# A chunked scan with a feed-forward block: turns as PE transposes, one turn of the keys, and the down products and v's projection placed differently

## The chip, the cores and the metric

The kernel runs on one core of one Trainium2 chip. The metric is the device time in microseconds (us), the median of several executions; lower is better.

## What is computed

```python
x = x + layernorm(attn(layernorm(x)))           # x: 2048 x 512, float32
x = x + layernorm(ffn(layernorm(x)))
# attn: 16 heads of 32; chunks of 16 tokens, one after the other, with a state S (32 x 32 per head)
q = silu(x @ Wq); k = normalised(x @ Wk); v = x @ Wv; beta = 2 * sigmoid(x @ Wbeta)
def step(S, (qi, ki, vi, ei)):
    kh = ki @ S;  kh_hat = normalised(kh);  g = w * kh_hat + b - (vi - ki)
    v_new = (g*w - mean(g*w) - kh_hat * mean(g*w * kh_hat)) * rstd
    A = tril(qi @ ki.T) * ei
    o = qi + layernorm(qi @ S - A @ v_new)
    S = S - (ki * ei).T @ v_new
o = normalised(o * sigmoid(x @ Wg1 @ Wg2)) * norm_w;  attn = o @ Wo
# ffn: weights rounded to float8_e4m3, I = 1536
ffn = ((silu((x @ gate_w) * gs) * ((x @ up_w) * us)) @ down_w) * ds
```

## The kernel before

The 2048 tokens are 16 tiles of 128 rows. A tile holds 8 chunks of the scan in a form where all heads of a chunk are computed at once, so the scan is 128 chunks in a row, each needing the state of the one before. `body(t, s, h)` is one tile; s is t's parity and h = t // 2. Each engine has its own copy of `body` with the order of its work written out by hand, chunk by chunk (j = 0 to 7). In tile t the kernel runs tile t's scan, the preparation of tile t + 1 (`prep_*`), what follows the scan for tile t - 1 (`post_*`) and t - 2 (`tail_*`), and the feed-forward block for pairs of tiles (`pair_*`, `ffn_*`, `fin_*`). A pair has 6 rounds; each tile from the fourth on does three (numbers 0, 1 and 2 in `ffn`). A round is `ffn_g` (gate, bank G), `ffn_u` in two parts (up, bank U4), silu on ScalarE (ACT), the product f and its high and low halves fh and fl, and then `ffn_down` for k = 0 and k = 1, one per tile of the pair, each of four matmuls of 512 columns (L587). After tile 15, five more passes through `body` drain the pipeline.

In each chunk TensorE (PE) does `read_state` (L491 and L500), then some other work, then `write_state` (L514 and L522), then some more other work. Between the read and the write VectorE (DVE) and GpSimd (POOL) compute v_new: statistics (L1254), a power on POOL (L1000), and in the end VX (L1290). PE's write waits for VX. DVE adds the state S (L1297) once L514 is done, and the next read waits for S. DVE's other work stands behind VX, ahead of S ("front" places), and behind S.

PE's other work, by chunk, before the change:

- j = 0: read; down k = 1 of the last tile's round 1; the turn of xn; gate and up of round 0; write; up, second part.
- j = 1: read; q; down k = 0 of the last tile's round 2; write; its down k = 1.
- j = 2: read; in odd tiles the two turns of the pair (`pair_xT`); k; write; the turn of q.
- j = 3: read; gate and up of round 1; write; up, second part.
- j = 4: read; v; write; down k = 0 of round 0.
- j = 5: read; down k = 1 of round 0; two turns of the keys; gate of round 2; write; `prep_beta` (L413 and L397).
- j = 6: read; the turn of d; up of round 2; the gate projection (L420); write; `prep_cen` (L426).
- j = 7: read; `post_wo` (L537); write; down k = 0 of round 1; `prep_brow` (L426).

A turn (`turn`, L405) is a 128 x 512 tile turned block by block: eight matmuls against the identity, each 64 output columns wide, four for each half of the array. The projections, the read and the write are in the same 64-wide form; the feed-forward matmuls (L554, L587) are 128 wide. The trace has two records for each float32 matmul of a turn or a projection (x16 for a turn) and one for each feed-forward matmul.

The keys are turned twice, into PA[0] ("kT2") and PA[1] ("kT1"). DVE turns PA[0] once more into kR (`prep_kR`, L1199), in front place of j = 5. ACT copies PA[1] into BDk in two halves (`prep_BDk`, L755): the first in j = 5 ahead of the chunk's output copy (`take_qh`, L810), the second behind fh (L704), the gate copies (L719 and L704) and bt (L729). PE's turn of d waits for bt. ACT's rT (L778) comes later, and `prep_cen` waits for it. v is projected into PA[1]; `prep_d` (L1216) reads it, after kn (L1210). In tiles 0 to 4 DVE, ACT and POOL also round the feed-forward weights, one unit per chunk (L1392 to L1402, L860, L862, L1086).

Of the kernel before, what the change touches and what calls it, by code (L numbers as in the profile page):

```python
# [14 lines left out]
P = 128  # L15
T, D = 2048, 512
# [63 lines left out]
def begun(n):  # L80

    return not isinstance(n, int) or n >= 0


def build(nc, x, wq, wk, wv, wo, wbeta, wg1, wg2, norm_w, ln_w, ln_b, gate_w, up_w, down_w,
# [15 lines left out]
    with ctx:  # L101
# [7 lines left out]
        Wq, Wk, Wv, Wo = (sb(n, KD * D) for n in ("Wq", "Wk", "Wv", "Wo"))  # L109
# [11 lines left out]
        ident = cst[:, C_ID:C_ID + P]  # L121
# [7 lines left out]
        qT, qR, thR = ([sb(f"{n}{s}", D) for s in range(2)] for n in ("qT", "qR", "thR"))  # L129
        rR, kR = sb("rR", D), sb("kR", D)  # L130
# [9 lines left out]
        Pw, u, g, t_ = (work[:, 64 * n:64 * (n + 1)] for n in range(4))  # L140
# [36 lines left out]
        PA, G, U4, Y = bank[2:4], bank[4], bank[5], bank[6:8]  # L177
# [20 lines left out]
        prep_v = Each(sem, "prep_v", "kss qR kn d kR bx rR em er eM thR")  # L198
        prep_a = Each(sem, "prep_a", "xnT q ksq qT g1 beta BDk rT th")
        prep_t = Each(sem, "prep_t", "xnT q k qT v kT2 kT1 g1 beta dT gate cen brow")  # L200
# [80 lines left out]
        def half_done(t, s, h):  # L281

            p, r = (h - 2, 3) if s else (h - 2, 0)
            return [(p, r)] if is_pair(p) else []
# [99 lines left out]
        def _(pe):  # L384
            mm = nc.tensor.matmul


            HALVES = (slice(0, 64), slice(64, P))

            def half(t, block, lo):  # L390

                return t[:, block * P + lo.start:block * P + lo.stop]

            def proj(dst, W, n, blocks=range(KD)):
                for k in blocks:
                    for lo in HALVES:
                        ins = mm(dst[lo, :], half(xnT, k, lo), W[:, k * n:(k + 1) * n],  # L397
                                 start=(k == 0), stop=(k == KD - 1), skip_group_check=True)
                return ins

            def turn(dst, src, one):

                for g in range(4):
                    for lo in HALVES:
                        ins = mm(dst[lo, g * P:(g + 1) * P], half(src, g, lo), ident, start=True, stop=True,  # L405
                                 skip_group_check=True)
                ins.then_inc(*one)

            def gate_in(b):

                for k in range(KD):
                    for lo in HALVES:
                        ins = mm(b[lo, 0:64], Wgb[:, k * DG:k * DG + 64], half(xnT, k, lo),  # L413
# [24 lines left out]
                proj(PA[0][:, :], Wq, D).then_inc(*prep_t.one("q"))  # L438

            def prep_beta(t):  # L440
                pe.wait_ge(*prep_v.at("kR", t))
                gate_in(PA[0])
                proj(PA[0][:, P:P + H], Wb, H).then_inc(*prep_t.one("beta"))

# [7 lines left out]

                turn(PA[1], qtok, prep_t.one("qT"))

            def prep_vv(t):
                pe.wait_ge(*prep_v.at("qR", t))
                proj(PA[1][:, :], Wv, D).then_inc(*prep_t.one("v"))

            def prep_kT(t):
                pe.wait_ge(*prep_v.at("d", t))  # L460
                turn(PA[0], kn, prep_t.one("kT2"))
                turn(PA[1], kn, prep_t.one("kT1"))

            def prep_dT(t):
# [12 lines left out]
            def prep_brow(t):  # L477
                pe.wait_ge(*prep_v.at("rR", t))
                fixed(PA[0][:, 0:P], C_REP, bx[:, :], prep_t.one("brow"))
# [97 lines left out]
            def ffn_down(p, r, k):  # L577
                if k == 0:
                    pe.wait_ge(*low(p, r))
                    if p == 0:  # L580
                        pe.wait_ge(*quantized(r // 2, 12))
                    if r == 0 and p > 0:
                        pe.wait_ge(fin_v.sem, fin_v.at("y1", p - 1))
                for q in range(RM):
                    m = RM * r + q
                    for part in (fh, fl):
                        ins = mm(Y[k][:, :], part[:, q * PAIR + k * P:q * PAIR + (k + 1) * P], DW[:, m * D:(m + 1) * D],  # L587
                                 start=(m == 0 and part is fh), stop=(m == MI - 1 and part is fl))
                if k == 1:
                    ins.then_inc(*down_t.one("dn"))  # L590

            def body(t, s, h):
                norm, prep, scan, post, tail = live(t)
                o = 1 - s
                ffn = rounds(t, s, h)
                for j in range(NC):
                    if scan:
                        read_state(t, j, s)

                    if j == 0:  # L600
                        for p, r in half_done(t, s, h):
                            ffn_down(p, r, 1)
                        if prep:
                            prep_xnT(t + 1)
                        if 0 in ffn:
                            ffn_g(*ffn[0])
                            ffn_u(*ffn[0], 0)
                    if j == 1:
                        if prep:
                            prep_q(t + 1)  # L610
                        for p, r in left_over(t, s, h):
                            ffn_down(p, r, 0)
                    if j == 2:
                        if s and is_pair(h - 1):
                            pair_xT(h - 1)
                        if prep:
                            prep_k(t + 1)
                    if j == 3 and 1 in ffn:
                        ffn_g(*ffn[1])
                        ffn_u(*ffn[1], 0)  # L620
                    if j == 4 and prep:
                        prep_vv(t + 1)
                    if j == 5:
                        if 0 in ffn:
                            ffn_down(*ffn[0], 1)
                        if prep:
                            prep_kT(t + 1)
                        if 2 in ffn:
                            ffn_g(*ffn[2])
                    if j == 6:  # L630
                        if prep:
                            prep_dT(t + 1)
                        if 2 in ffn:
                            ffn_u(*ffn[2], 0)
                            ffn_u(*ffn[2], 1)
                        if prep:
                            prep_gate(t + 1)
                    if j == 7 and post:
                        post_wo(t - 1)
                    if scan:  # L640
                        write_state(t, j, s)

                    if j == 0 and 0 in ffn:
                        ffn_u(*ffn[0], 1)
                    if j == 1:
                        for p, r in left_over(t, s, h):
                            ffn_down(p, r, 1)
                    if j == 2 and prep:
                        prep_qT(t + 1)
                    if j == 3 and 1 in ffn:  # L650
                        ffn_u(*ffn[1], 1)
                    if j == 4 and 0 in ffn:
                        ffn_down(*ffn[0], 0)
                    if j == 5 and prep:
                        prep_beta(t + 1)
                    if j == 6 and prep:
                        prep_cen(t + 1)
                    if j == 7:
                        if 1 in ffn:
                            ffn_down(*ffn[1], 0)  # L660
                        if prep:
                            prep_brow(t + 1)

            def prologue():

# [34 lines left out]
        def _(act):  # L700
# [44 lines left out]
            def prep_BDk(t, s, a):  # L745

                if a == 0:
                    act.wait_ge(*prep_t.at("kT1", t))
                    if begun(NC * (t - 1) - 1):
                        act.wait_ge(scan_t.sem, scan_t.at("kh", NC * (t - 1) - 1))  # L750
                for h in (2 * a, 2 * a + 1):
                    q = slice(32 * h, 32 * h + 32)
                    for gp in range(2):
                        p = 64 * gp + 32 * (h % 2)
                        ins = fn(bdk(s)[q, :, gp, own(h)],  # L755
                                 PA[1][p:p + 32, 256 * a:256 * a + 256].rearrange("p (m c) -> p m c", c=CH), ACT.Copy)
                if a or t == 0:
                    ins.then_inc(*prep_a.one("BDk"))
# [407 lines left out]
        def _(dve):  # L1166
# [30 lines left out]
            def turn(dst, src, one):  # L1197

                nc.vector.transpose(rows(dst), feat(src)).then_inc(*one)  # L1199
# [16 lines left out]
                tt(dv[:, :], kn[:, :], PA[1][:, :], ALU.subtract).then_inc(*prep_v.one("d"))  # L1216

            def prep_kR(t, s):
                dve.wait_ge(*prep_t.at("kT2", t))
                if begun(t - 1):  # L1220
                    dve.wait_ge(kdiag_a.sem, kdiag_a.at("k3", t - 1))
                turn(kR, PA[0], prep_v.one("kR"))

            def prep_rR(t, s, b=PA[0]):
                dve.wait_ge(*prep_t.at("cen", t))
# [383 lines left out]
```

## Time and profile before

| what | value |
|---|---|
| median of 3 runs | 943.51 us (943.5 to 944.17) |
| the profiled execution | 944.36 us, span 942.60 us |
| PE busy | 840.1 us, 89% of the span |
| DVE, ACT, POOL busy | 670.3, 505.2, 482.6 us |
| chain that ended last | PE 63%, DVE 17%, POOL 10%, ACT 5%, issue 4% |
| mean granted TensorE clock | 0.959 |

The span is that of the profiled execution, from the first to the last instruction. In a timeline row the columns are the start, the length from the first start to the last end of what was merged, engine, line, operation, output<-inputs, shape and count; in brackets stands how long the engine was idle before it and what released it. Matmuls overlap, so the time from one start to the next is what counts, not a record's length. The L514 row of a chunk is its write, the L491 row its read.

### The profile page before, as it was taken

To read this page: it belongs to the slowest core of one execution; us is meant where nothing else is said; L and a number is where in the kernel's file an instruction comes from. 1 tells how busy PE (TensorE), PEld (TensorE's weight loads), DVE (VectorE), ACT (ScalarE), POOL (GpSimd) and SP (SyncE) were. 2 spreads that over 40 slices of the span, in tenths; PEclk is the share of its full clock that TensorE was granted. 3 is DMA by queue.
4 is the path that set the end of the run, shared out by engine and by line. 5 is a ranking of instruction groups with operands and counts; after the bars stand their busy time and mean duration, and the time that the engine had idled before them with its cause. 6 is when DMAs were issued, how large, how long until landed. Compare 5 with 4: busy or idle time off the path is not lost.

```text
span 942.6 us, 25277 instructions
## 1 busy us (share of the span) xinstructions
PE 840.1 (89%) x9472; PEld 595.6 (63%) x9472; DVE 670.3 (71%) x2695; ACT 505.2 (54%) x1330; POOL 482.6 (51%) x858
## 2 busy tenths in 40 slices
PE   6777676688989999999999999999999999979795
PEld 2444343456567676677576776766676767667594
DVE  2587887978877778677776777677876777767332
ACT  1667575766646565554556464655555564633222
POOL 4355645565554646455555546464555546436312
PEclk9897888989989999999999999999999999989998
DMA  7011121111200001000100010000100010001000
GB/s 257 15 53 48 46 69 34 53 51 35 68 13 24 2 2 46 6 20 2 45 2 24 1 45 4 25 2 2 47 2 24 2 46 2 2 2 45 1 23 23
DMA packets 16730, 28.63 MB, mean 30 GB/s; under 512 B 3520, under 2 KB 3520, under 8 KB 16608
## 3 DMA queue, kind: packets, MB, share of 16 engines
q1 hardware_dynamic: 16608, 27.02, 8.9%
q8 instruction: 75, 1.23, 0.5%
q14 instruction: 47, 0.39, 0.1%
HBM read 22.82 MB, written 4.19 MB: 29 GB/s over the span
## 4 chain that ended last, share of the span: by engine, by line
PE 63%; DVE 17%; POOL 10%; ACT 5%; issue 4%; DMA 0%; POOLq 0%; DVEq 0%; ACTq 0%
PE bank L554 16%; PE bank L397 14%; PE bank L587 9%; PE bank L405 7%; PE bank L514 4%; PE bank L537 4%; POOL rho L1000 3%; PE bank L491 2%; PE bank L522 2%; PE bank L500 2%; DVE work L1281 2%; PE bank L426 1%; DVE work L1285 1%; PE bank L420 1%; DVE VX L1290 1%
## 5 line engine op out<-in xcount | busy, mean ns | idle before, releaser
L1000 POOL TENSOR_TENSOR rho<-sy,cst 128x2 f32<-128x2 f32 x128 | 89.7, 701 | 284.9 <-DVE sy L1254 284.9
L1297 DVE TENSOR_TENSOR SQ<-SQ,bank 128x128 f32<-128x128 f32 x128 | 36.8, 288 | 110.4 <-PE bank L514 109.8
L514 PEld LDWEIGHTS bank<-VX,BDkR 128*64 128x64 f32 x1024 | 45.9, 142 | 96.7 <-issue 51.8
L514 PE MATMUL bank<-VX,BDkR 128*64 128x64 f32 x1024 | 57.7, 235 | 49.9 <-DVE VX L1290 48.7
L810 ACT ACTIVATE qhR<-bank 128x64 f32<-128x64 f32 x128 | 28.3, 221 | 112.0 <-PE bank L522 111.8
L587 PE MATMUL bank<-DW,fh 128*128 128x512 f32 x192 | 84.4, 440 | 1.5 <-DVE fl L1364 1.5
L769 ACT ACTIVATE BDkR<-kR,cst 128x128 f32<-128x128 f32 x256 | 81.4, 398 | 0.0
L587 PE MATMUL bank<-DW,fl 128*128 128x512 f32 x192 | 76.3, 397 | 0.0
L1081 POOL TENSOR_TENSOR fl<-f,fh 128x512 fp32r<-128x512 f32 x32 | 45.6, 1425 | 53.0 <-ACT fh L704 32.3
L1276 DVE SCALAR_TENSOR_TENSOR work<-work,rho,rR 128x32 f32<-128x32 f32 x256 | 53.0, 249 | 25.4 <-POOL rho L1000 24.9
L554 PE MATMUL bank<-xh,GW 128*128 128x256 f32 x384 | 66.3, 296 | 2.8 <-DVE xl L1347 2.5
L755 ACT ACTIVATE BDk<-bank 32x256 f32<-32x256 f32 x124 | 46.5, 375 | 41.5 <-PE bank L405 40.1
L554 PE MATMUL bank<-xh,UW 128*128 128x256 f32 x384 | 66.0, 294 | 0.3 <-DVE f L1358 0.3
L397 PE MATMUL bank<-Wq,xnT 128*64 128x512 f32 x256 | 64.3, 647 | 0.0
L491 PEld LDWEIGHTS bank<-SQ,BDk 128*64 128x64 f32 x1024 | 45.7, 142 | 29.5 <-issue 26.3
L554 PE MATMUL bank<-xl,GW 128*128 128x256 f32 x384 | 62.8, 287 | 0.0
L397 PE MATMUL bank<-Wv,xnT 128*64 128x512 f32 x256 | 62.5, 633 | 0.0
L537 PE MATMUL bank<-Wo,o 128*64 128x512 f32 x256 | 59.9, 611 | 2.9 <-DVE o L1329 2.9
L491 PE MATMUL bank<-SQ,BDk 128*64 128x48 f32 x1024 | 55.8, 231 | 6.5 <-DVE SQ L1297 4.7
L397 PE MATMUL bank<-Wk,xnT 128*64 128x512 f32 x256 | 60.5, 616 | 0.7 <-ACT xnT L704 0.7
L554 PE MATMUL bank<-xl,UW 128*128 128x256 f32 x384 | 61.0, 281 | 0.0
L500 PE MATMUL bank<-SQ,BDq 128*64 128x32 f32 x1024 | 53.2, 225 | 7.9 <-ACT qhR L810 6.7
(154 smaller groups left out, 2224.8 us busy)
## 6 DMA issues: line engine op xcount, KB each, us to landing
xt<-in_x SPq DMA_DIRECT2D x16, 256.0 KB, 2.7
x<-in_x SPq DMA_DIRECT2D x16, 256.0 KB, 2.8
out<-x SPq DMA_DIRECT2D x16, 256.0 KB, 2.0
yb<-in_gate_w SPq DMA_DIRECT2D x12, 256.0 KB, 2.7
yb<-in_up_w SPq DMA_DIRECT2D x12, 256.0 KB, 2.7
yb<-in_down_w SPq DMA_DIRECT2D x12, 256.0 KB, 2.6
Wk<-in_wk SPq DMA_DIRECT2D x1, 1024.0 KB, 6.3
Wv<-in_wv SPq DMA_DIRECT2D x1, 1024.0 KB, 8.2
```

What stands on the lines that cost most here:

```text
L397: ins = mm(dst[lo, :], half(xnT, k, lo), W[:, k * n:(k + 1) * n], start=(k == 0), stop=(k == KD - 1), skip_group_check=True)
L405: ins = mm(dst[lo, g * P:(g + 1) * P], half(src, g, lo), ident, start=True, stop=True, skip_group_check=True)
L491: ins = mm(KAv[gp * 64:(gp + 1) * 64, gh, 0:48], bdk(s)[:, gh * NC + j, gp, :], SQv[:, 2 * gh + gp, :], start=True, stop=True, skip_group_ ...
L500: ins = mm(QH[gp * 64:(gp + 1) * 64, gh * DH:(gh + 1) * DH], bdq[:, j // 4, 2 * gp + gh, j % 4, :], S[:, 2 * gh + gp, :], start=(gh == 0), ...
L514: ins = mm(dS[p, e], bdkr[:, gh, j % 4, p], VX[:, e], start=True, stop=True, skip_group_check=True)
L537: ins = mm(PA[1][lo, :], half(ogT, g, lo), Wo[:, g * D:(g + 1) * D], start=(g == 0), stop=(g == 3), skip_group_check=True)
L554: ins = mm(b[:, q * PAIR:(q + 1) * PAIR], W[:, k * I + m * P:k * I + (m + 1) * P], part[:, k * PAIR:(k + 1) * PAIR], start=(part is xh and ...
L587: ins = mm(Y[k][:, :], part[:, q * PAIR + k * P:q * PAIR + (k + 1) * P], DW[:, m * D:(m + 1) * D], start=(m == 0 and part is fh), stop=(m ...
L755: ins = fn(bdk(s)[q, :, gp, own(h)], PA[1][p:p + 32, 256 * a:256 * a + 256].rearrange("p (m c) -> p m c", c=CH), ACT.Copy)
L769: ins = fn(bdkr[:, :, place, h * DH:(h + 1) * DH], kR[:, :].rearrange("p (gh j e) -> p gh j e", gh=2, e=DH)[:, :, js], ACT.Identity, scale ...
L1000: tt(dst, src, cst[:, C_NH:C_NH + n], ALU.pow).then_inc(*one)
L1276: stt(out=g2(g)[:, gh], in0=g2(u)[:, gh], scalar=rho[:, gh:gh + 1], in1=r_j[:, gh, :], op0=ALU.mult, op1=ALU.add).then_inc(*scan_v.one(f"g ...
```

## The change

- `turn` on PE becomes four `transpose` instructions, 128 x 128 each, over the whole array.
- The keys are turned once in the loop, into PA[1]. DVE's `prep_kR` reads PA[1] for t > 0, and ACT's `prep_BDk` waits for kR (t > 0) before its first half. `prep_beta` on PE waits for kn instead of kR. The prologue turns the keys twice as before.
- `ffn_down` k = 0 of round 1 moves from behind the write of j = 7 to behind the read of the next j = 0, directly ahead of k = 1; that of round 0 from behind the write of j = 4 to behind the read of j = 5, ahead of k = 1.
- v's projection takes its first three quarters where it was (j = 4, before the write) and the last one behind the write of j = 4.

```diff
             def turn(dst, src, one):
                 for g in range(4):
-                    for lo in HALVES:
-                        ins = mm(dst[lo, g * P:(g + 1) * P], half(src, g, lo), ident, start=True, stop=True,
-                                 skip_group_check=True)
+                    ins = nc.tensor.transpose(dst[:, g * P:(g + 1) * P], src[:, g * P:(g + 1) * P], ident)
                 ins.then_inc(*one)
...
             def prep_beta(t):
-                pe.wait_ge(*prep_v.at("kR", t))
+                pe.wait_ge(*prep_v.at("kn", t))
...
-            def prep_vv(t):
-                pe.wait_ge(*prep_v.at("qR", t))
-                proj(PA[1][:, :], Wv, D).then_inc(*prep_t.one("v"))
+            def prep_vv(t, last):
+                if last:
+                    proj(PA[1][:, :], Wv, D, (3,)).then_inc(*prep_t.one("v"))
+                else:
+                    pe.wait_ge(*prep_v.at("qR", t))
+                    proj(PA[1][:, :], Wv, D, (0, 1, 2))
             def prep_kT(t):
                 pe.wait_ge(*prep_v.at("d", t))
-                turn(PA[0], kn, prep_t.one("kT2"))
                 turn(PA[1], kn, prep_t.one("kT1"))
...
                     if j == 0:
                         for p, r in half_done(t, s, h):
+                            ffn_down(p, r, 0)
                             ffn_down(p, r, 1)
...
                     if j == 4 and prep:
-                        prep_vv(t + 1)
+                        prep_vv(t + 1, False)
                     if j == 5:
                         if 0 in ffn:
+                            ffn_down(*ffn[0], 0)
                             ffn_down(*ffn[0], 1)
...
-                    if j == 4 and 0 in ffn:
-                        ffn_down(*ffn[0], 0)
+                    if j == 4 and prep:
+                        prep_vv(t + 1, True)
...
-                    if j == 7:
-                        if 1 in ffn:
-                            ffn_down(*ffn[1], 0)
-                        if prep:
-                            prep_brow(t + 1)
+                    if j == 7 and prep:
+                        prep_brow(t + 1)
... ScalarE, prep_BDk
                 if a == 0:
                     act.wait_ge(*prep_t.at("kT1", t))
+                    if t > 0:
+                        act.wait_ge(*prep_v.at("kR", t))
... VectorE
             def prep_kR(t, s):
-                dve.wait_ge(*prep_t.at("kT2", t))
+                dve.wait_ge(*prep_t.at("kT1" if t else "kT2", t))
...
-                turn(kR, PA[0], prep_v.one("kR"))
+                turn(kR, PA[1] if t else PA[0], prep_v.one("kR"))
```

## Rows read from the trace of the kernel before

**Rows 1.** Timeline of PE, tile 9: read and write of chunk 0

```profile
503.36 0.39 PE L491 MATMUL bank<-SQ,BDk 128*64 128x48 f32 x8
...
509.07 0.45 PE L514 MATMUL bank<-VX,BDkR 128*64 128x64 f32 x8
```

**Rows 2.** Timeline, tile 9, chunk 3: VX and the write

```profile
528.67 0.29 DVE L1290 TENSOR_TENSOR VX<-work,re 128x128 f32<-128x128 f32 x1
...
529.02 0.45 PE L514 MATMUL bank<-VX,BDkR 128*64 128x64 f32 x8 [0.57 <-DVE VX L1290]
```

**Rows 3.** Timeline, tile 9: write of chunk 7, state, read of tile 10

```profile
554.11 0.45 PE L514 MATMUL bank<-VX,BDkR 128*64 128x64 f32 x8 [0.32 <-DVE VX L1290]
...
554.61 0.29 DVE L1297 TENSOR_TENSOR SQ<-SQ,bank 128x128 f32<-128x128 f32 x1
...
556.10 0.39 PE L491 MATMUL bank<-SQ,BDk 128*64 128x48 f32 x8
```

**Rows 4.** Timeline of PE, tile 9: write of chunk 2, turn, read

```profile
523.38 0.40 PE L514 MATMUL bank<-VX,BDkR 128*64 128x64 f32 x8
...
523.82 1.07 PE L405 MATMUL bank<-cst,q_kn_th 128*64 128x128 f32 x16
524.72 0.39 PE L491 MATMUL bank<-SQ,BDk 128*64 128x48 f32 x8
```

**Rows 5.** Timeline of PE, tile 9: write of chunk 4, down product, read

```profile
534.70 0.40 PE L514 MATMUL bank<-VX,BDkR 128*64 128x64 f32 x8
...
535.23 0.50 PE L587 MATMUL bank<-DW,fh 128*128 128x512 f32 x1
535.57 0.40 PE L587 MATMUL bank<-DW,fl 128*128 128x512 f32 x1
...
536.04 0.40 PE L587 MATMUL bank<-DW,fl 128*128 128x512 f32 x1
536.37 0.44 PE L491 MATMUL bank<-SQ,BDk 128*64 128x48 f32 x8
```

**Rows 6.** Groups of instructions, PE's weight loads (busy us, mean ns)

```profile
L405 PEld LDWEIGHTS bank<-cst,q_kn_th 128*64 128x64 f32 x768 | 41.6, 137 | 9.0 <-issue 4.0 <-DVE xn_dv_rT L1216 2.7 <-DVE q_kn_th L1515 1.5
L587 PEld LDWEIGHTS bank<-DW,fl 128*128 128x128 f32 x192 | 36.5, 190 | 4.9
```

**Rows 7.** Timeline, tile 9, front of chunk 4: v and VX

```profile
531.23 3.63 PE L397 MATMUL bank<-Wv,xnT 128*64 128x512 f32 x16
...
533.50 0.29 DVE L1290 TENSOR_TENSOR VX<-work,re 128x128 f32<-128x128 f32 x1
```

**Rows 8.** Timeline, tile 9, chunks 4 to 6: keys, ACT's queue, turn of d

```profile
536.07 0.69 DVE L1216 TENSOR_TENSOR xn_dv_rT<-q_kn_th,bank 128x512 f32<-128x512 f32 x1
...
539.70 0.29 DVE L1290 TENSOR_TENSOR VX<-work,re 128x128 f32<-128x128 f32 x1
539.91 0.71 DVE L1199 STREAM_TRANSPOSE kR<-bank 128x512 f32<-128x512 f32 x1
...
540.11 1.54 ACT L755 ACTIVATE BDk<-bank 32x256 f32<-32x256 f32 x4 [3.00 <-PE bank L405]
...
542.88 0.62 ACT L704 ACTIVATE fh<-f 128x512 fp32r<-128x512 f32 x1
...
543.68 0.21 ACT L719 ACTIVATE g1T<-bank 32x64 f32<-32x64 f32 x1 [0.18 <-PE bank L397]
...
544.15 0.18 ACT L729 ACTIVATE bt<-bank 128x16 f32<-128x16 f32 x1
...
544.38 1.09 PE L405 MATMUL bank<-cst,xn_dv_rT 128*64 128x128 f32 x16 [0.27 <-ACT bt L729]
...
548.40 0.40 PE L514 MATMUL bank<-VX,BDkR 128*64 128x64 f32 x8
```

**Rows 9.** Stretches of 10 us: length, PE, PEld, DVE, ACT, POOL, PEclk, DMA share, GB/s

```profile
80.00:90.00 10.00, 7.94 (x65) 4.85 (x64) 8.29 (x37) 6.93 (x17) 5.47 (x9) 0.52 0.25 79
...
820.00:830.00 10.00, 6.46 (x105) 5.08 (x104) 8.21 (x36) 6.82 (x20) 7.44 (x13) 1.00 0.00 1
```

## The prediction, made before the changed kernel was run

> **What bounds the kernel now.** I read the PE timeline of one steady tile first, then the other engines in the same stretch, then the granted clock. Call the time from a chunk's first read matmul (L491) to its first write matmul (L514) its front, and from there to the next read its post; C0 to C7 are the chunks of a tile. Every piece of feed-forward and preparation work sits in a front or a post, so each slot ends either when PE is through or when the scan's own chain is. The mark is in the L514 row: with "<-DVE VX" and an idle time, the chain ended last; with no idle time, PE did. In C0 of tile 9 there is no idle time [rows 1], and none in C4 and C6, whose writes stand further down: PE ends them last. In C3 and C7 PE waited 0.57 and 0.32 us for VX [rows 2, 3]. L514 follows the start of VX by 0.35 us (528.67 to 529.02) [rows 2]. Tile 9 takes 52.7 us (503.36 to 556.10) [rows 1, 3]. It is a chain of slots, so I price the change slot by slot and give a slot only what its other bound allows.
>
> **Unit prices.** A turn in C2's post takes 0.90 us, from 523.82 to the next read at 524.72 [rows 4]. Of a down product (four matmuls) one matmul follows the other in 0.23 us (535.57 to 536.04 is two) [rows 5]. Going from 64-wide to 128-wide work costs something: L514 to the next work is 0.44 us where that is a 64-wide turn (523.38 to 523.82) and 0.53 where it is a down product (534.70 to 535.23), the first down matmul holds 0.34 instead of 0.23, and the last one 0.33 (536.04 to 536.37) [rows 4, 5]. So an excursion into 128-wide work costs 0.09 + 0.11 + 0.10 = 0.30 us beside its work.
>
> **The transposes.** No row shows one. A turn becomes four of them, each a 128-column weight load and 128 moving columns. The load of 64 columns has a record of 137 ns and that of 128 columns one of 190 [rows 6]: 53 ns per 64 columns, so 107 ns for 128, and the rest of a record overlaps. I take one load after the other as the pace: 4 x 0.107 is 0.43, with starts 0.45 us a turn, against 0.90. Lower end: only the streaming counts, a quarter of a down matmul's 0.23 each, 0.23 us a turn. Upper end: nothing overlaps, 4 x (0.19 + 0.06) = 1.0 us. The value nearest a row of the same thing, a 128-column load, is 0.45. The Trainium skill, "TensorE: Matmul & The Clock Gate", Terms, says transpose mode is 4 times faster for FP32. That would be an estimate of 0.22 us a turn and about 901 us in all; I see the load bound as the reason to stay above it, and the sum does not use the page.
>
> **Slot by slot, steady tiles.** Each is after minus before; tau = 0.45 is the turn.
> - *C7 post* loses down k=0 of round 1. 554.11 to 556.10 was 1.99 us; what is left for PE is the write and brow. The state addition S starts 0.50 after the write and takes 0.29 [rows 3], so with the hand-over the floor is about 0.89: -1.10.
> - *C0 front* takes that product: +0.93. Its turn goes from 0.90 to 0.45, and since that turn now is 128-wide, between a down product and gate matmuls, one excursion vanishes, -0.30. Together +0.18. PE ended it last, and stays so. DVE, which waited for brow, gets it earlier: no loss.
> - *C2 front*, odd tiles only: the pair's two turns, 1.80, become 0.90, but stand 128-wide between 64-wide work, +0.30: -0.60. PE ended it last.
> - *C2 post*: one turn shorter, -0.45 + 0.30. I cost it at nothing: C3 ends with VX, and VX hangs on DVE's queue from S on, and in even tiles on the keys' squares; what PE saves it waits for in C3 [rows 2].
> - *C4 front*: v's last quarter goes. v takes 531.23 to 534.70, 3.47 us, a quarter 0.87. The chain allows a write 0.35 after VX starts, 533.85, so 0.85 of it is gained [rows 7]: -0.85. These two bounds are then within 0.02 us of each other.
> - *C4 post to C6 write*, as one stretch of 13.70 us (534.70 to 548.40) [rows 5, 8]. PE's part: the post holds v's quarter, 0.87, instead of a product with an excursion, 1.23: -0.36. C5's front: +0.93 for the product, -1.80 for two turns, +0.45 for one, -0.30 for the excursion: -0.72. So PE could reach dT's turn, which it did 0.27 before 544.38, or 9.41 after the write, at 8.33. But ACT now holds it. **New waits:** d (L1216) started 1.37 us after the write; v's last matmul now ends 0.44 + 0.87 + 0.16 (the record's 3.63 against 3.47) later, so d moves by some 0.1 to 0.15, and with it VX, to 5.15. kR starts 0.21 after VX and takes 0.71; today BDk's first half (540.11) runs beside kR, afterwards it must wait for it: 6.1 instead of 5.41. Behind it on ACT are the output copy, fh, the gate copies and bt: 1.54 for BDk, about 0.1, fh 0.62, then 0.47 from the first gate copy to bt and 0.23 from bt to the turn [rows 8]. dT's turn starts 9.1 after the write, not 9.68: -0.58, and PE idles 0.75 us instead of 0.27. From there on 4.02 us less 0.45: -0.45. The stretch: -1.03. Beta's matmuls now wait for kn instead of kR; kn is over before d starts, so this costs nothing.
> - C0's post, C1, C5's post, C6's post and C7's front keep their times.
>
> An odd and an even tile: 2 x 0.18 - 0.60 - 2 x 1.10 - 2 x 0.85 - 2 x 1.03 = -6.2 us (-3.4 and -2.8). Written with tau it is 6 tau - 8.9. Tiles 5 to 14 are five such pairs: -31.
>
> **The rest.** Tile 4 has no cover for C4 (weights are still being quantised on DVE): 0.18 - 1.03 - 1.10, about -2.0. Tile 3 has the first rounds in it: its C7's post, -1.1, and 0.2 at its turns: -1.3. In tiles 0 to 2 the chain ends the slots; there ACT also works on the quantising, and I add 0.5 each, +1.5, an estimate: the 0.7 by which BDk starts later, less some slack. Tile 15 has no preparation: the product moved into C0 costs 0.93, C4's post gains about 1.1: -0.2. Before the first chunk five turns stand on the path, 5 x 0.45: -2.3. The last pair's two turns, after the scan: -0.9. Sum of these -5.2; all together **-36 us**. The profiled execution took 944.36 us (span 942.60), 0.85 above the median of 943.51; from it the sum gives 908.4, from the median 907.5. I take 907.5.
>
> **Rivals.**
> - *Turns cost what they did* (tau 0.9: full-width, but no cheaper). 5 x (6 x 0.9 - 8.9) = -17.5, and the rest gives -2.9 only, without the prologue's part: 923. Even then one turn and the excursions are gone. For it: nothing in the trace shows a transpose. Against it: half its loads are gone. 0.10.
> - *Only streaming counts* (tau 0.23): 5 x -7.5 = -37.5 and -6: 900. 0.12.
> - *ACT becomes the bound around C5 and C6*: the wait for kR also delays the output copy that C6's second read needs, and everything behind it. If the stretch gives nothing back (1.03 x 11 tiles) and early tiles lose 1 us more each, 907.5 + 11.3 + 3 = 922. 0.07.
> - *Slower: the clock falls in the steady stage.* PE's granted clock is 0.52 in 80 to 90 us, with PE at 7.94 of 10, and 1.00 in 820 to 830 with PE at 6.46 [rows 9]: busy share alone does not tell, but PE would be less busy than today. The two levels are 1.2 and 2.4 GHz; each us of PE work done at the lower one costs a half to one more. In tile 9 PE worked 51.5 us (52.7 less 0.57, 0.32 and 0.27), and the sum takes 4.2 of turns and excursions out: 47.3 in 49.3. The gain is 3.1 a tile, so the change turns into a loss once more than 3.1 us a tile of its work, 6 to 7%, falls to the lower level; with a fifth of each steady tile there it would be 907.5 + 10 x 9.5 = 1002. Against it: those 47.3 of 49.3, with 0.75 us as the longest wait. 0.04. The Trainium skill, "TensorE: Matmul & The Clock Gate", Part 4, says that transposes do not count as PE being busy, which would be this rival's mechanism; a tile has 5 or 6 turns of 0.45 us, never more than two together, with matmuls on both sides.
> - *It all cancels*, within 0.2% (what a measurement of this kernel can tell from no change): 0.02; it would need tau at 1.0 and the ACT bound together.
>
> **How the numbers follow.** The forecast case has 0.65, the rivals 0.10, 0.12, 0.07, 0.04 and 0.02. Its own spread is about 8 us either way, from starts between unlike matmuls and from tiles 0 to 4. The range runs from 897, below the streaming case, to 926, above the 923 and the 922; the end at tau 1.0, 5 x (6 - 8.9) - 2, is 927. Faster 0.94, same 0.02, slower 0.04.
>
> **What the profile of the changed kernel would show.** Turns as records 128*128 128x128, four each, next work 0.45 us later; 81 turns, not 96. A C7 post of 0.9 us; C0's front 5.9; C4's front 3.1; an idle time of 0.7 to 0.8 us ahead of dT's turn "<-ACT bt" for 0.27; BDk starting just after kR; tile 9 in 49.3 us. I am wrong in the turn if that spacing is not 0.4 to 0.5, in the slot model if two tiles don't shorten by 8.9 - 6 tau, and in the whole if PEclk shows less than full speed between 300 and 800 us.

## The result, and the profile after

| | before | changed |
|---|---|---|
| median, us | 943.84 (943.5 to 944.41, 4 runs) | 920.49 (918.7 to 924.58, 4 runs) |
| ratio, 95% interval | 1 | 0.9758 [0.9723, 0.9793] |
| profiled execution, span | 944.36, 942.60 | 919.38, 917.6 |
| mean granted clock | 0.959 | 0.938 |

Faster by 23.4 us where 36 was forecast: the direction and the range held, a third of the gain is missing. The range held for a reason that is partly luck: the forecast case had a spread of 8 us around 907.5, and 920.49 lies outside it; what reaches that far are the ends put there for the rivals at 922 and 923. The page of the changed kernel, parts 1 (busy time), 4 (the chain that ended last) and two groups of part 5:

```profile
PE 797.5 (87%) x8260; PEld 558.3 (61%) x8260; DVE 671.1 (73%) x2695; ACT 500.9 (55%) x1330; POOL 481.6 (52%) x858
...
PE 51%; DVE 20%; POOL 11%; ACT 9%; issue 7%; DMA 1%; SPq 0%; POOLq 0%; DVEq 0%; ACTq 0%
...
L758 ACT ACTIVATE BDk<-bank 32x256 f32<-32x256 f32 x124 | 46.5, 375 | 62.0 <-DVE kR L1202 52.6
...
L502 PE MATMUL bank<-SQ,BDq 128*64 128x32 f32 x1024 | 54.9, 228 | 15.0 <-ACT qhR L813 14.0
```

PE lost 42.6 us of busy time but the program only 25, and PE's share of the last chain fell from 63% to 51%, ACT's rose from 5% to 9%: work left PE and waits on ACT came in. The last two rows name them: BDk waits for kR, as forecast, and PE's second read (L502) waits for qhR, which was not.

**The turn**, answering [rows 4]. Timeline of PE around tile 9's chunk 2, start and length in us:

```profile
509.91 1.09 PE L405 MATMUL bank<-cst,xn 128*128 128x128 f32 x8
510.93 3.65 PE L398 MATMUL bank<-Wk,xnT 128*64 128x512 f32 x16
...
514.42 0.40 PE L516 MATMUL bank<-VX,BDkR 128*64 128x64 f32 x8
...
514.96 0.66 PE L405 MATMUL bank<-cst,q_kn_th 128*128 128x128 f32 x4
515.54 0.44 PE L493 MATMUL bank<-SQ,BDk 128*64 128x48 f32 x8
```

Two turns take 1.02 us to the next 64-wide work and one takes 0.58. The difference is one turn without its excursion: 0.44, and 0.58 - 0.44 = 0.14 is left for leaving 128-wide work; entering it costs 0.54 instead of 0.44 after the write (514.42 to 514.96). So an excursion costs 0.10 + 0.14 = 0.24. Forecast: 0.45 a turn and 0.30 an excursion. The weight loads, answering [rows 6], stretch 300 to 800 us (busy, mean ns):

```profile
L405 PEld LDWEIGHTS bank<-cst,q_kn_th 128*128 128x128 f32 x80 | 9.2, 140 | 1.8
```

The record of a 128-column load is 140 ns here, not the 190 of [rows 6], and the pace is 0.44 / 4 = 0.11 us a transpose. The matmul turn with its 64-column loads kept the same pace: 0.90 / 8 = 0.11 us a step. The transposed turn has half as many steps.

**Chunk 0**, answering [rows 1], PE timeline: tile 9 (odd) and, further down, tile 10 (even) with the write and state before it, answering [rows 3]:

```profile
494.79 0.44 PE L493 MATMUL bank<-SQ,BDk 128*64 128x48 f32 x8
...
500.71 0.45 PE L516 MATMUL bank<-VX,BDkR 128*64 128x64 f32 x8
...
543.24 0.45 PE L516 MATMUL bank<-VX,BDkR 128*64 128x64 f32 x8 [0.32 <-DVE VX L1293]
...
543.74 0.29 DVE L1300 TENSOR_TENSOR SQ<-SQ,bank 128x128 f32<-128x128 f32 x1
...
544.17 0.44 PE L493 MATMUL bank<-SQ,BDk 128*64 128x48 f32 x8
...
544.25 0.19 POOL L1012 TENSOR_TENSOR nb_y<-nm_y,rs_y 128x1 f32<-128x1 f32 x1
...
544.47 0.72 ACT L840 ACTIVATE x<-x,nb_y 128x512 f32<-128x512 f32 x1 [0.46 <-POOL nb_y L1012]
...
545.10 0.20 ACT L813 ACTIVATE qhR<-bank 128x64 f32<-128x64 f32 x1
...
545.45 0.42 PE L502 MATMUL bank<-SQ,BDq 128*64 128x32 f32 x8 [0.84 <-ACT qhR L813]
...
551.13 0.45 PE L516 MATMUL bank<-VX,BDkR 128*64 128x64 f32 x8
```

The post of C7 is 544.17 - 543.24 = 0.93 us, as forecast (0.89). The front of C0 is 5.92 in the odd tile (forecast 5.89) but 6.96 in the even one. In an even tile ACT's queue holds the second half of fin_yc (L840, the pair's closing normalization) ahead of chunk 7's qhR. L840 waits for nb_y on POOL, which ends at 544.44; qhR runs behind it, and PE, whose read now begins 1 us earlier than it used to, stands 0.84 us at L502. The same place before the change, behind the write of 554.11 [rows 3]:

```profile
555.35 0.72 ACT L837 ACTIVATE x<-x,nb_y 128x512 f32<-128x512 f32 x1 [0.46 <-POOL nb_y L1009]
...
555.98 0.20 ACT L810 ACTIVATE qhR<-bank 128x64 f32<-128x64 f32 x1
...
556.33 0.42 PE L500 MATMUL bank<-SQ,BDq 128*64 128x32 f32 x8
```

qhR started 1.87 us after the write before and 1.86 after the change, the second read 2.22 and 2.21. In an even tile nothing of what C7's post gave up was left at the second read.

**Chunks 3 to 6 of tile 9**, timeline of PE, DVE and ACT, answering [rows 2, 5, 7, 8]:

```profile
519.71 0.29 DVE L1293 TENSOR_TENSOR VX<-work,re 128x128 f32<-128x128 f32 x1
...
520.06 0.45 PE L516 MATMUL bank<-VX,BDkR 128*64 128x64 f32 x8 [0.57 <-DVE VX L1293]
...
521.79 0.44 PE L493 MATMUL bank<-SQ,BDk 128*64 128x48 f32 x8
...
524.54 0.29 DVE L1293 TENSOR_TENSOR VX<-work,re 128x128 f32<-128x128 f32 x1
...
524.98 0.45 PE L516 MATMUL bank<-VX,BDkR 128*64 128x64 f32 x8
...
526.33 0.42 PE L493 MATMUL bank<-SQ,BDk 128*64 128x48 f32 x8
...
530.48 0.71 DVE L1202 STREAM_TRANSPOSE kR<-bank 128x512 f32<-128x512 f32 x1
...
531.28 1.53 ACT L758 ACTIVATE BDk<-bank 32x256 f32<-32x256 f32 x4 [4.24 <-DVE kR L1202]
...
533.91 0.18 ACT L730 ACTIVATE bt<-bank 128x16 f32<-128x16 f32 x1
...
534.15 0.66 PE L405 MATMUL bank<-cst,xn_dv_rT 128*128 128x128 f32 x4 [0.62 <-ACT bt L730]
```

C4's front is 3.19 (was 3.95), its post 1.35 (1.67), BDk starts 6.30 after C4's write and 0.09 behind kR's end, and dT's turn starts 9.17 after it, with 0.62 us idle ahead of it (forecast 9.1 and 0.75).

**The clock**, answering [rows 9]. Two stretches of the changed kernel (length, busy PE, PEld, DVE, ACT, POOL, PEclk, DMA share, GB/s), and the first one before, where PEclk was 0.88:

```profile
30.00:250.00 220.00, 159.29 (x1692) 101.32 (x1692) 169.12 (x671) 141.58 (x353) 117.49 (x187) 0.80 0.17 48
...
300.00:800.00 500.00, 480.64 (x5257) 339.23 (x5255) 393.04 (x1662) 285.55 (x807) 279.37 (x523) 1.00 0.06 17
```

```profile
30.00:250.00 220.00, 163.65 (x2020) 107.11 (x2022) 172.42 (x683) 144.27 (x363) 119.02 (x190) 0.88 0.16 49
```

Full in the steady stage, lower in the early tiles. By stretches of the profiled executions, cut at the read of each C0, in us:

| | before | changed | difference | forecast |
|---|---|---|---|---|
| up to the first read | 31.04 | 30.62 | -0.4 | -2.3 |
| tiles 0 to 2 | 152.61 | 156.02 | +3.4 | +1.5 |
| tiles 3, 4 | 55.97, 58.19 | 56.06, 56.70 | +0.1, -1.5 | -1.3, -2.0 |
| tiles 5 to 14 | 514.22 | 489.15 | -25.1 | -31 |
| tile 15 and the end | 130.57 | 129.05 | -1.5 | -1.1 |

### The profile page after: what moved, and what is told of

Read it like the earlier page. It is cut to its first block, busy times and chain, and to the rows that moved or that the text cites. A ratio compares the mean times of both kernels' runs of the same rounds, so it can differ in the third digit from the quotient of the medians.

```text
span 917.6 us, 22854 instructions
## 1 busy us (share of the span) xinstructions
PE 797.5 (87%) x8260; PEld 558.3 (61%) x8260; DVE 671.1 (73%) x2695; ACT 500.9 (55%) x1330; POOL 481.6 (52%) x858
## 3 DMA queue, kind: packets, MB, share of 16 engines
q8 instruction: 65, 1.06, 0.5%
## 4 chain that ended last, share of the span: by engine, by line
PE 51%; DVE 20%; POOL 11%; ACT 9%; issue 7%; DMA 1%; SPq 0%; POOLq 0%; DVEq 0%; ACTq 0%
PE bank L398 14%; PE bank L556 13%; PE bank L589 7%; POOL rho L1003 4%; PE bank L516 4%; PE bank L539 4%; ACT BDk L758 2%; PE bank L405 2%; PE bank L493 2%; DVE work L1284 2%; DVE f L1361 2%; PE bank L502 2%; DVE work L1288 1%; PE bank L524 1%; PE bank L419 1%
## 5 line engine op out<-in xcount | busy, mean ns | idle before, releaser
L589 PE MATMUL bank<-DW,fh 128*128 128x512 f32 x192 | 82.3, 428 | 1.9 <-DVE fl L1367 1.9
L1279 DVE SCALAR_TENSOR_TENSOR work<-work,rho,rR 128x32 f32<-128x32 f32 x256 | 53.0, 249 | 25.6 <-POOL rho L1003 25.1
L502 PE MATMUL bank<-SQ,BDq 128*64 128x32 f32 x1024 | 54.9, 228 | 15.0 <-ACT qhR L813 14.0
L398 PE MATMUL bank<-Wv,xnT 128*64 128x512 f32 x256 | 67.5, 650 | 0.0
```

What stands on the lines that cost most here:

```text
L502: ins = mm(QH[gp * 64:(gp + 1) * 64, gh * DH:(gh + 1) * DH], bdq[:, j // 4, 2 * gp + gh, j % 4, :], S[:, 2 * gh + gp, :], start=(gh == 0), ...
L1279: stt(out=g2(g)[:, gh], in0=g2(u)[:, gh], scalar=rho[:, gh:gh + 1], in1=r_j[:, gh, :], op0=ALU.mult, op1=ALU.add).then_inc(*scan_v.one(f"g ...
```

## The experiments

Ratios are to the kernel before on the same chip, with a 95% interval. Edits are to the changed kernel unless "to before" is said.

**1. Transposes alone** (to before: the turn's body is the changed one, all work where it was).

```
-    for lo in HALVES:
-        ins = mm(dst[lo, g * P:(g + 1) * P], half(src, g, lo), ident, ...)
+    ins = nc.tensor.transpose(dst[:, g * P:(g + 1) * P], src[:, g * P:(g + 1) * P], ident)
```

> The kernel before with its turns as transposes and nothing else changed. Theory (slot sum, with the 0.44 us a turn that the changed kernel shows): C0 -0.75 (turn -0.45, one excursion -0.30), C5 -1.2 (two turns and an excursion), C6 -0.45, C2 -0.6 in odd tiles: 2.7 us a tile, 27 over tiles 5 to 14, 3 to 4 more in tiles 3, 4 and the drain, and the tiles before lose some 2 to 3 us to a lower clock: about 915 us, no slower than the whole change, and no wait of L500 for qhR in C0. Rival A: the gain of 23 us is made by the moves and the single turn of the keys, the transposes being hidden: 935 or more. Rival B: the slot sum holds for the parts, so this gives less than the whole, 922 to 928.

916.71 us (915.38 to 918.03), 0.9714 [0.9698, 0.973]. The transposes alone bring the whole gain of the change: tiles 5 to 14 go from 514.22 to 488.04 us, and the rest of the change makes them 1.1 us longer (489.15). In the steady tiles C5's front went from 5.67 to 4.46 (two turns), C6's from 4.93 to 4.30, and C0's in odd tiles from 5.71 to 5.28. C0 was expected to give 0.75 and gave 0.43, since its write now waits 0.29 us for VX: PE is through before the chain. The down product that the full change moves there partly fills this gap, and C0's front becomes 5.92, 0.64 more and not 0.93.

**2. The moves alone** (the changed kernel's order, each turn as eight 64-wide matmuls again).

```
-    ins = nc.tensor.transpose(dst[:, g * P:(g + 1) * P], src[:, g * P:(g + 1) * P], ident)
+    for lo in HALVES:
+        ins = mm(dst[lo, g * P:(g + 1) * P], half(src, g, lo), ident, ...)
```

> The changed kernel with its turns as the 64-wide matmuls of before. Theory: C7's post -1.06, C0 +0.93 and in even tiles 0.85 more for the output copy held up on ScalarE, C4 -0.76 and -0.31, C5 0, C6 +0.35 for the wait for bt: -0.85 in odd and about 0 in even tiles, so 937 to 941 us. Rival A (moves make the gain): 925 or less. The granted clock from 30 to 250 us tells whether the transposes lower it: theory 0.88 as before, rival 0.80 as in the changed kernel.

941.32 us (938.73 to 943.61), 0.9969 [0.9954, 0.9984]: the key turn that is left out and the three moves bring 0.3% together, and with matmul turns tiles 5 to 14 take 508.21 us, 6.0 less than before. Gains of the parts don't add up: 26.2 and 6.0 apart, 25.1 together. Experiments 3, 5 and 6 take them one by one.

**3. The two down products alone** (to before: ffn_down of k=0 beside its other slices in C0's and C5's fronts, nothing behind the writes of C4 and C7).

```
+    ffn_down(p, r, 0)
     ffn_down(p, r, 1)
...
+    ffn_down(*ffn[0], 0)
     ffn_down(*ffn[0], 1)
...
-    if j == 4 and 0 in ffn:
-        ffn_down(*ffn[0], 0)
...
-    if 1 in ffn:
-        ffn_down(*ffn[1], 0)
```

> The kernel before with the down products of rounds 0 and 1 whole (k = 0 ahead of k = 1 in C0 and C5), nothing else. Theory: C7's post -1.06, C0 +0.93 in odd and +1.9 in even tiles (the output copy held up behind L840), C4's post -0.75 (S sets the floor), C5 +0.93: about 0 in odd and +1 in even tiles, 943 to 949 us, no gain and perhaps a loss. Rival (saved excursions are the gain, 0.30 each and two a tile): 936 to 938.

949.23 us (946.68 to 950.96), 1.0049 [1.0037, 1.0061]: alone this part is a loss, of 0.5%. Its waits of PE, 300 to 800 us (total us, times, longest), show the new one at L500, the second read:

```profile
PE bank L514 <- DVE VX L1287: 5.1, 12, 0.6
PE bank L500 <- ACT qhR L807: 4.3, 5, 0.9
```

The product behind C4's write was partly free. A post cannot be shorter than the state addition allows, 0.88 us here in C4: taking the product out shortens C4's post by 0.78 and lengthens C5's front by 0.95. In C7 1.06 leave the post (1.99 to 0.93) and 0.96 arrive in C0's front in odd tiles, but 1.99 in even ones: it becomes 6.67 and 7.74 (before 5.71 and 5.75). So a pair of tiles loses 1.2 us, nearly all of it by the wait for qhR, which the prediction did not have.

**4. qhR ahead of the second normalization** (ACT's queue in chunk 7: L840 of the second half stands behind take_qh).

```
-                            fin_yc(2 * (h - 2) + 1, 1)
...
+                    if j == 7 and fin:
+                        fin_yc(2 * (h - 2) + 1, 1)
```

> The changed kernel with the second of the two ScalarE instructions L840 (fin_yc, which waits for nb_y) placed behind chunk 7's output copy instead of ahead of it. Theory: in even tiles C0's 0.84 us wait of the second read for qhR goes, C0 falls from 6.96 to about 6.0, 7 tiles have it, so 6 us less than the changed kernel: 914 to 915. Rival: C0 in even tiles is held by something behind it (the copy of fh, the output store), and the time stays at 920.

915.14 us (912.76 to 915.52), 0.9688 [0.9671, 0.9704], 5.3 below the changed kernel's 920.49. PE's waits of the changed kernel from 299 to 789 us, then of this one from 300 to 784:

```profile
PE bank L405 <- ACT bt L730: 6.2, 10, 0.6
PE bank L516 <- DVE VX L1293: 6.0, 15, 0.6
PE bank L502 <- ACT qhR L813: 4.4, 6, 0.8
```

```profile
PE bank L405 <- ACT bt L730: 6.3, 10, 0.6
PE bank L516 <- DVE VX L1294: 6.0, 15, 0.6
...
PE bank L502 <- ACT qhR L813: 0.2, 1, 0.2
```

Only the wait for qhR is gone; C0's front is 5.92 in every tile, and tiles 5 to 14 take 483.95 us. That is 30.3 less than before: the -31 that was forecast.

**5. The keys turned twice again** (a second turn into PA[0], kR from it, no wait for kR ahead of BDk, beta's matmuls behind kR).

```
+                turn(PA[0], kn, prep_t.one("kT2"))
...
-                    if t > 0:
-                        act.wait_ge(*prep_v.at("kR", t))
```

> The changed kernel with the keys turned twice again (kR from PA[0], ScalarE's first half of BDk not waiting for kR, beta's matmuls waiting for kR), all turns transposes. Theory: C5 +0.44 for the second turn, C6 back from 4.84 to 4.30 because dT's turn no longer waits 0.62 us for bt: -0.1 us a tile, so the single turn of the keys is worth nothing here, 918 to 921 us in all; tiles 0 to 2 stay near 155 us because their loss is the clock's. Rival (the wait for kR costs more than what the slots show, in tiles 0 to 3 above all): 914 or less. Rival (the single turn brings what it saves on PE): 924 or more.

916.26 us (915.11 to 918.26), 0.9691 [0.967, 0.9713]. By the median it is 2 to 4 us shorter than the changed kernel, which gave 920.49 and 918.39 in two measurements, and below the 918 to 921 that was expected. The profile has tiles 5 to 14 at 489.32 us against 489.15, with 1.5 us of it in a single late C0 of tile 14, and tile 3 at 55.00 against 56.06. C5's front pays the turn, 4.94 to 5.37, and C6's gives 4.84 to 4.29 back, since BDk no longer waits for kR and bt comes earlier. Together -0.12 a tile: to turn the keys once gains nothing here, since what PE saves in C5 it waits for in C6.

**6. v whole in C4's front** (the last quarter not behind the update).

```
-                if last:
-                    proj(PA[1][:, :], Wv, D, (3,)).then_inc(*prep_t.one("v"))
-                else:
+                if not last:
...
-                    proj(PA[1][:, :], Wv, D, (0, 1, 2))
+                    proj(PA[1][:, :], Wv, D).then_inc(*prep_t.one("v"))
```

> The changed kernel with all of v's projection ahead of C4's write again, so that C4's post holds nothing but the write. Theory: C4's front 3.19 to 3.95, its post 1.35 to the floor of 0.88 that the state addition sets: +0.3 us a tile, some 3 us in all over the changed kernel. Rival (the last quarter delays d and with it VX and kR, and that costs as much): no difference, within 1 us.

923.99 us (923.58 to 924.8), 0.9797 [0.978, 0.9813]. Beside it the **changed kernel was measured again**:

> The changed kernel itself once more, beside the one above on the same chip. Theory: its early tiles run at a clock that differs from execution to execution, so 917 to 924 us, a spread of 0.5%, with the steady tiles 5 to 14 at 489 us in every one. Rival: the 4 us between it and the kernel that turns the keys twice come from the runs, and it gives 916 here.

918.39 us (917.35 to 923.82), 0.9752 [0.9726, 0.9777], the ratio of the result again. So the moved quarter is worth 5.6 us by the medians and 494.10 - 489.15 = 5.0 in tiles 5 to 14. C4's front goes from 3.95 to 3.19 and its post from 0.88 to 1.35: of the quarter's 0.87 us, 0.76 leave the front and 0.47 come back in the post, whose floor hides the rest. C6's front, 5.01 here, is 4.84 with the move; the expected 3 us had no such term.

**7. qhR early, and bt ahead of fh** (experiment 4, and in C5 of ACT the gate copies and bt stand ahead of fh).

```
+                        if prep:
+                            prep_g1(t + 1)
...
-                            prep_g1(t + 1)
```

> The changed kernel with ScalarE reordered at two places: the second L840 behind chunk 7's output copy, and in C5 fh behind the gate copies and bt. Theory: C0 of even tiles -1.04 as measured before, and dT's 0.62 us wait for bt goes except for some 0.1, so C6 falls from 4.85 to 4.3 in each of ten tiles: 5 us less than with the first alone, 909 to 910. Rival: fh, 0.7 us later, makes GpSimd's fl late for C0's first down product, or beta's matmuls end too late for it, and it stays at 914 to 915.

908.79 us (906.62 to 910.31), 0.9615 [0.9592, 0.9637]; tiles 5 to 14 take 479.33 us, 4.6 less than in experiment 4. ACT's part of C5, the same rows as at 531.28 above:

```profile
474.50 1.54 ACT L758 ACTIVATE BDk<-bank 32x256 f32<-32x256 f32 x4 [4.24 <-DVE kR L1204]
...
476.62 0.18 ACT L730 ACTIVATE bt<-bank 128x16 f32<-128x16 f32 x1
476.70 0.62 ACT L705 ACTIVATE fh<-f 128x512 fp32r<-128x512 f32 x1
```

bt follows BDk's start by 2.12 us instead of 2.63, and between 300 and 780 us the wait at L405 is no longer among PE's waits. BDk still waits for kR 4.24 us, and that costs PE nothing now.

**8. Matmul turns for the early tiles** (the turns that prepare tiles 1 to 4 are 64-wide matmuls).

```
-                turn(PA[0], xn, prep_t.one("xnT"))
+                turn(PA[0], xn, prep_t.one("xnT"), t <= 4)
```

(and so for the turns of q, kn and d)

> The changed kernel with the turns of tiles 1 to 4 (the ones prepared while PE has idle time) as 64-wide matmuls again; all later ones stay transposes. Theory (early tiles lost time to a lower clock): the mean granted clock from 30 to 250 us rises from 0.80 towards 0.88, tiles 0 to 2 come out 2 to 3 us shorter although their turns are dearer, 917 to 919. Rival (ScalarE's wait for kR is what tiles 0 to 2 lost): clock or not, tiles 0 to 2 keep their 156 us and the time stays at 920 to 922.

917.35 us (916.57 to 920.29), 0.9722 [0.9702, 0.9742]. Tiles 0 to 2 take 153.95 us instead of 156.02, with a granted clock of 0.84 instead of 0.80 between 30 and 250 us: PE does more work, and the stretch is shorter. The medians alone can't show it: 917.35 lies 1.0 below the repeat of the changed kernel, within the spread of its runs.

**9. The early tiles with both key turns** (experiment 7, with the early matmul turns of 8 and, for tiles 1 to 3, a second turn of kn into PA[0] that nobody reads; the computed result doesn't change).

```
+                if t <= 3:
+                    for g in range(4):
+                        for lo in HALVES:
+                            mm(PA[0][lo, g * P:(g + 1) * P], half(kn, g, lo), ident, ...)
```

> The reordered kernel with 64-wide matmul turns in the preparation of tiles 1 to 4, and in tiles 1 to 3 a second turn of the keys into PA[0] that nobody reads, only to keep TensorE at work in C5. Theory (the clock falls in C5 of tiles 0 to 2 because TensorE does too little there): C5's post in tiles 0 to 2 goes back from 2.58 to 1.58 us, the granted clock from 30 to 250 us to 0.86 to 0.88, tiles 0 to 2 to about 153 us; 3 us less than with the reordering alone: 906 to 907. Rival (these tiles wait for ScalarE behind kR): C5's post may fall but C6 takes it back, tiles 0 to 2 stay at 154 or more, and the time at 908 to 910.

905.28 us (904.46 to 906.94), 0.9582 [0.9563, 0.96]: the fastest version of this study. Tiles 0 to 2 take 152.39 us against 155.76 in experiment 7, the steady tiles the same as there (479.35). C5's post is 1.42 us in each of the three tiles; it was 2.58 in experiment 7 and 1.58 before the change. PE in C5 of tile 1, first in the changed kernel, then here:

```profile
118.49 0.69 PE L516 MATMUL bank<-VX,BDkR 128*64 128x64 f32 x8 [2.94 <-DVE VX L1293]
...
119.36 1.10 PE L412 MATMUL bank<-xnT,Wgb 128*64 128x64 f32 x16
120.25 0.99 PE L398 MATMUL bank<-Wgb,xnT 128*64 128x16 f32 x16
121.07 0.65 PE L493 MATMUL bank<-SQ,BDk 128*64 128x48 f32 x8
```

```profile
116.41 0.45 PE L526 MATMUL bank<-VX,BDkR 128*64 128x64 f32 x8 [1.63 <-DVE VX L1305]
...
116.90 0.67 PE L417 MATMUL bank<-xnT,Wgb 128*64 128x64 f32 x16
117.39 0.60 PE L398 MATMUL bank<-Wgb,xnT 128*64 128x16 f32 x16
117.83 0.42 PE L503 MATMUL bank<-SQ,BDk 128*64 128x48 f32 x8
```

Two stretches of the changed kernel around that write (columns as in the clock's windows):

```profile
119.30:121.00 1.70, 1.70 (x38) 1.70 (x36) 1.56 (x4) 1.57 (x5) 1.17 (x1) 0.50 0.02 5
117.00:118.70 1.70, 0.21 (x4) 0.21 (x6) 1.66 (x10) 0.48 (x1) 1.62 (x4) 0.87 0.30 110
```

In the changed kernel PE had stood 2.94 us before the write (busy 0.21 of 1.70 us), and the matmuls behind it ran at a granted clock of 0.50, the lower level of 1.2 GHz: C5's post is 2.58 us, against 1.42 here, where PE stood 1.63 us after the second turn and had 1.00. From 30 to 250 us the mean is 0.87 here and 0.81 in experiment 7.

## Why the prediction was right and where it failed

**The turn: its price right, its reason not shown.** 0.44 us against 0.45. I had derived it from the 190 ns record of a 128-column load; the transposes' record is 140 ns, and the matmul turn kept the same 0.11 us a step with 64-column loads. So the price was in part luck, and no run tells what sets the pace. The bounds 0.23 and 1.0 are both excluded, and with them the rival in which turns cost the same (923 was near the time by chance: in experiment 1 the turns gained 27 us). The Trainium skill, "TensorE: Matmul & The Clock Gate", Terms, gives a factor of 4 for FP32 in transpose mode; the rows show a turn falling from 0.90 to 0.44, a factor of 2, and here the measurement decides.

**The slots of odd tiles: right.** Tile 9 took 49.38 us (forecast 49.3). Term by term: C7's post -1.06 (forecast -1.10); C0's front +0.21 (+0.18); C2's front -0.60 (-0.60); C2's post -0.2 and C3 +0.2 (0 together); C4's front -0.76 (-0.85); C4's post -0.32 (-0.36); C5's front -0.73 (-0.72); C4's write to C6's write 12.55 against 13.69, -1.14 (-1.03); the new wait ahead of dT 0.62 (0.75), with its stated cause, kR to BDk to bt. By the prediction's own sign the slot model still failed: two tiles should have shortened by 8.9 - 6 tau, 6.3 us with tau at 0.44, and shortened by 5.1.

**The step that failed: "C0 front ... Together +0.18", in even tiles.** There it was +1.21 (5.75 to 6.96), so that a pair gained 5.1 and not 6.2: 5 x 1.03 = 5.2 of the missing us. I priced C0's front by PE's work alone and wrote "DVE, which waited for brow, gets it earlier: no loss", but never asked what ACT had to deliver for the second read. The removed product was the cover of qhR behind L840. The prediction gave C7's post only what its other bound allows and took the state addition for that bound; the next bound, the arrival of qhR at the second read, was left out. Experiment 4 takes exactly this wait out and gets the 5 us.

**The prologue, -2.3, came as -0.4** in the profiled execution. The turn of xn is 0.9 us shorter, but Wk landed 8.3 us after its issue instead of 6.3, so PE started the key projection at 10.08, behind "<-DMA Wk", instead of 9.49. In the repeat Wk took 6.7 us and the first read came at 28.62, 2.4 earlier than before; in experiment 1 at 28.78. The term is about right when Wk is on time, and Wk's landing (6.2 to 9.0 us over these profiles) was not in the sum at all.

**Tiles 0 to 2, +1.5, came as +3.4, and tile 3, -1.3, as +0.1.** In tiles 0 to 2 the sign was right and the mechanism was not the one priced, which was ACT's wait for kR. Without that wait they took as long (156.51 in experiment 1, 156.05 in experiment 5), and experiment 9 gives 3.4 us back (152.39 against 155.76) with the wait in place; what changed there is PE's work and its clock. C5's post shows where: 1.58 us in each of the three tiles before, 2.58, 2.58 and 2.53 in the changed kernel, which is 2.95 of the 3.4. For tile 3 the profile has a part of the answer. Its C6 front went from 4.92 to 6.67 us: the second read waits 0.64 for qhR and the turn of d 0.56 for bt, both behind BDk, which waits for kR, and the granted clock from 232 to 234 us, behind these waits, is 0.50. Without the wait for kR (experiment 5) this front is 4.29, its post 2.28 instead of 1.32, and tile 3 takes 55.00.

**The sum.** Of the 36 us the profiled executions lack 11.2: 5.9 in tiles 5 to 14 (5.2 of it the wait for qhR), 1.9 each ahead of the first read and in tiles 0 to 2, 1.4 in tile 3 and 0.5 in tile 4, while the end gave 0.4 more than forecast.

**The rivals.** That ACT becomes the bound: half true. In tile 3 it came at the place named, in the steady tiles at another. ACT's queue cost 0.62 us a tile at bt, which was in the sum, and 1.03 a pair at qhR, which was not; experiment 7 shows that both together were worth about 10 us. That the clock falls in the steady stage: it stayed at 1.00, with PE busy 480.6 of 500 us. It did fall in the early tiles, where I had no such term. Tiles 0 to 2 and the granted clock from 30 to 250 us, by the turns of the keys in C5 (the other turns are of the same kind; in experiment 8 those of tiles 1 to 4 only):

| turns | two of the keys | one of the keys |
|---|---|---|
| matmuls | 152.61, 0.88 (before) | 153.71, 0.84 (experiment 2), 153.95, 0.84 (8) |
| transposes | 156.51, 0.81 (experiment 1) | 156.02, 0.80 (changed) |

With two matmul turns again (experiment 9) it is 152.39 and 0.87; with two transposed turns and the other moves (experiment 5) 156.05 and 0.81. So the kind of turn goes with 2.1 to 3.9 us, and the second matmul turn, with the moves or the reordering in it, with 1.1 to 1.6. The Trainium skill, the same page, Part 4, says that transpose mode doesn't count as PE-busy the same way. These numbers fit the page, but transposes also keep PE at work for half as long, and no run keeps the time equal; the cause stays open between the two. One count of the prediction was off: a tile has four turns, six in odd tiles, not 5 or 6.

## What to carry to other kernels

When work is taken out of a slot, list what every other engine delivers at the slot's end and in the next one, queue by queue: here a down product of 1 us behind the state update was the cover for one ACT instruction that stood behind another which waited for POOL, and reordering ACT's queue in two places (experiment 7) gave another 11.7 us, half of what the whole change gave. A product behind an update whose floor is set elsewhere is partly free; move it only if something else fills that floor. Where an early stage has PE idle and its clock below full, PE work taken out can lengthen it, so such stages deserve a decision of their own.

## What the runs showed of the hardware

- At a granted clock of 1.00 a 128x128 FP32 transpose with its weight load keeps a pace of 0.11 us, and a turn of four costs half of what its eight 64-wide matmuls cost; beside 128-wide feed-forward work the hand-over is smaller still (0.35 us from the start of the turn in tile 9's C0 to the gate matmuls behind it). The record of its weight load is 140 ns where that of the down products' is 188.
- Added PE work shortened a stage: a turn that nobody reads, together with matmul turns in place of transposes, gave 1.42 instead of 2.58 us in C5's post, and 3.4 us over three tiles.
- The same DMA of Wk landed between 6.2 and 9.0 us after its issue in the twelve profiles, of kernels that issue it alike.
